# Stores of the normalised pairs issued from ScalarE's queue instead of SyncE's, in a fused graph-layer kernel

## What is computed

```python
msg  = x[src]
agg  = segment_sum(msg, dst)              # sum over the edges that end in a node
mean = agg / max(deg, 1)
h    = mean @ W_l + b + x @ W_r
y    = x + h * sigmoid(h)
out  = (y - mean(y)) / sqrt(var(y) + 1e-5)   # per node, over its 512 features
```

## Time and profile before

| what | value |
|---|---|
| median of 3 runs | 1533.49 us |
| the profiled execution's own time | 1532.49 us |
| its span, first to last instruction | 1530.7 us |
| PE, DVE, ACT, POOL busy, share of the span | 98, 86, 77, 67% |
| mean granted TensorE clock | 0.995 |
| device memory traffic over the span | 309 GB/s |

### The profile page before, as it was taken

The page is one execution under the profiler, slowest core; times in us unless marked ns, Lnnn a source line. Parts: engine busy times, 40 slices in busy tenths (PEclk is TensorE's granted clock), DMA queues, the critical chain, the costliest instruction groups (busy, mean ns, idle before and its releaser), DMA issues.

```text
span 1530.7 us, 23969 instructions
## 1 busy us (share of the span) xinstructions
PE 1498.7 (98%) x7198; PEld 1240.8 (81%) x7198; DVE 1320.3 (86%) x2090; ACT 1180.0 (77%) x1603; POOL 1025.4 (67%) x1089
## 2 busy tenths in 40 slices
PE   8999999999999999999999999999999999999996
PEld 6887778888888778888888888888888888888885
DVE  7988999999997878888888888888888888887886
ACT  5454333333334889999999999999999999999997
POOL 6446566666662766766767767667777777777774
PEclk9999999999999999999999999999999999999998
DMA  6476688989987789999989999999999999999996
GB/s 208 156 223 189 203 253 266 267 260 264 268 267 214 205 251 287 287 276 278 276 263 298 274 283 282 277 280 270 277 285 270 279 275 288 289 274 270 291 271 199
DMA packets 299349, 397.68 MB, mean 260 GB/s; under 512 B 43036, under 2 KB 145206, under 8 KB 299221
## 3 DMA queue, kind: packets, MB, share of 16 engines
q1 hardware_dynamic: 252277, 321.93, 70.5%
q0 software_dynamic: 46944, 74.22, 18.0%
HBM read 333.87 MB, written 139.67 MB: 309 GB/s over the span
## 4 chain that ended last, share of the span: by engine, by line
PE 68%; ACT 8%; issue 8%; DMA 5%; DVE 5%; POOL 5%; SPq 0%; POOLq 0%; ACTq 0%; DVEq 0%
PE pH L546 61%; DMA cor<-correction_rows,node_idx 4%; PE pT L651 3%; PE pT L620 3%; ACT cor L755 2%; ACT O L808 2%; POOL cor L452 2%; ACT pH L823 1%; ACT Z L835 1%; POOL rstd L516 1%; POOL var_eps L513 1%; PE pT L557 1%; POOL light_cor L452 1%; DVE Z L914 1%; DVE xs L1102 0%
## 5 line engine op out<-in xcount | busy, mean ns | idle before, releaser
L452 POOL DMA_INDIRECT cor<-correction_rows,node_idx x347 | 396.1, 1141 | 241.6 <-ACT cor L755 138.7
L546 PE MATMUL pH<-ws_hi,x_hi 128*128 128x512 f32 x876 | 347.3, 396 | 6.2 <-ACT pH L823 2.5
L546 PE MATMUL pH<-ws_hi,x_lo 128*128 128x512 f32 x876 | 343.3, 392 | 0.0
L546 PE MATMUL pH<-ws_lo,x_hi 128*128 128x512 f32 x876 | 342.3, 391 | 0.0
L546 PE MATMUL pH<-wb_hi,x_hi 128*128 128x512 f32 x688 | 275.5, 400 | 1.4 <-DVE x_lo L1090 1.3
L546 PE MATMUL pH<-wb_hi,x_lo 128*128 128x512 f32 x688 | 268.3, 390 | 0.0
L546 PE MATMUL pH<-wb_lo,x_hi 128*128 128x512 f32 x688 | 267.9, 389 | 0.0
L808 ACT ACTIVATE O<-Z,shift,rstd 128x512 f32<-128x512 f32 x347 | 262.7, 808 | 2.0 <-DVE shift L1137 1.9
L1127 DVE BATCH_NORM_STATS2 stats<-Z 128x6 f32<-128x512 f32 x347 | 219.4, 674 | 0.0
L729 ACT ACTIVATE s_hi<-sums 128x512 fp32r<-128x512 f32 x98 | 62.1, 634 | 196.8 <-issue 163.7
L1119 DVE TENSOR_TENSOR Z<-Z,X 128x1024 f32<-128x1024 f32 x174 | 211.3, 1214 | 1.1 <-ACT Z L835 1.1
(11 more groups left out here) (147 smaller groups left out, 2758.5 us busy)
## 6 DMA issues: line engine op xcount, KB each, us to landing
X<-in_x SPq DMA_DIRECT2D x173, 512.0 KB
out<-O SPq DMA_DIRECT2D x173, 512.0 KB
xs<-in_x SPq DMA_DIRECT2D x344, 128.0 KB
correction_rows<-c_out SPq DMA_DIRECT2D x98, 256.0 KB
light_x<-in_x SPq DMA_DIRECT2D x51, 256.0 KB, 2.9
light_h<-early_product SPq DMA_DIRECT2D x44, 256.0 KB
out<-light_o SPq DMA_DIRECT2D x44, 256.0 KB
join_row<-joined SPq DMA_DIRECT2D x98, 64.0 KB
```

What stands on the lines that cost most here:

```text
L452: g.indirect_dma_start(out=out_, out_offset=None, in_=table, in_offset=bass.IndirectOffsetOnAxis(ap=idx, axis=0), bounds_check=bound, oob_ ...
L546: last = mm(ps, a[:, k], w[:, k], start=(n == 0 and not onto), stop=(n == len(terms) - 1), skip_group_check=onto)
```

## The change

The function `store_out` moves, with its wait, from SyncE's block to ScalarE's. SyncE issued the store of pair t-3 in step t, after X's load. ScalarE issues the store of pair t-4 in step t, after the seed of pair t+1 and before `reset_cor` of pair t+3. At that place the normalisation of pair t-4 is the last instruction of ScalarE's step before. Behind the last step the stores stand between what is left of the normalisations.

```diff
 # SyncE
-            def store_out(t, q, u):
-                nt, rows = pair_shape(t)
-                b = u % 2
-                wait(sp, normed, t + 1)
-                if nt == 2:
-                    sp.dma_start(out[bass.ds(BASE + t * 2 * P, 2 * P), :].rearrange("(a p) n -> p a n", p=P), O[:, b]
-                                 ).then_inc(stored[b], 16)
...
                 shifted(t, q, u, 3, NP, load_x)
-                shifted(t, q, u, -3, NP, store_out)
                 lights(light, t)
             peeled(0, NP, move)
-            single(NP - 3, store_out)
-            single(NP - 2, store_out)
             last_lights(light)
-            single(NP - 1, store_out)
 # ScalarE
+            def store_out(t, q, u):
...
+                wait(act, normed, t + 1)
+                if nt == 2:
+                    act.dma_start(out[bass.ds(BASE + t * 2 * P, 2 * P), :].rearrange("(a p) n -> p a n", p=P), O[:, b]
+                                 ).then_inc(stored[b], 16)
...
                 if t + 1 >= ADDED:
                     shifted(t, q, u, 1, NP, seed)
+                shifted(t, q, u, -4, NP, store_out)
                 shifted(t, q, u, 3, NP, reset_cor)
                 lights(light, t)
                 shifted(t, q, u, -3, NP, normalise)
             peeled(0, NP, node_pair)
+            single(NP - 4, store_out)
             single(NP - 3, normalise)
             single(NP - 1, silu)
+            single(NP - 3, store_out)
             single(NP - 2, normalise)
             last_lights(light)
+            single(NP - 2, store_out)
             single(NP - 1, normalise)
+            single(NP - 1, store_out)
```

More of the change, by code:

```diff
@@ L353, in load_blocks @@
                                  ).then_inc(blocks_in, 16)
-            def store_out(t, q, u):
-                nt, rows = pair_shape(t)
-                b = u % 2
-                wait(sp, normed, t + 1)
-                if nt == 2:
-                    sp.dma_start(out[bass.ds(BASE + t * 2 * P, 2 * P), :].rearrange("(a p) n -> p a n", p=P), O[:, b]
-                                 ).then_inc(stored[b], 16)
-                else:
-                    sp.dma_start(out[BASE + t * 2 * P:N, :], O[0:rows, b, 0]).then_inc(stored[b], 16)
             def load_light(l):
@@ L835, in silu @@
                 a_(Z[0:rows, b, 0:nt], h, ACT.Silu).then_inc(silu_made, 1)
+            def store_out(t, q, u):
+                nt, rows = pair_shape(t)
+                b = u % 2
+                wait(act, normed, t + 1)
+                if nt == 2:
+                    act.dma_start(out[bass.ds(BASE + t * 2 * P, 2 * P), :].rearrange("(a p) n -> p a n", p=P), O[:, b]
+                                 ).then_inc(stored[b], 16)
+                else:
+                    act.dma_start(out[BASE + t * 2 * P:N, :], O[0:rows, b, 0]).then_inc(stored[b], 16)
             def light_make_silu(l):
```

## The result

The changed kernel takes 1528.32 us (median of 10 runs, 1527.06 to 1529.98) against 1532.14 us for the kernel before (10 runs, 1529.29 to 1535.54): ratio 0.9974, interval 0.9966 to 0.9982. Three more measurements on other occasions gave 0.9976, 0.9977 and 0.9979. So it is faster by 0.21 to 0.26%, some 3 to 4 us. In the last of these measurements 2 of 12 executions of the changed kernel took 1724 and 1879 us at a mean granted clock of 0.82 and 0.75 instead of 0.995, and are left out of its ratio. The forecast of 1533.7 us was wrong, in its sign as in its range.

A forecast was written before the change was run, and what follows sets the result against it. PE's pace through its instruction list was taken to bound the pair stage, with ScalarE second at 0.23 us slack a step. Terms 0 + 0 + 0 + 0.2 us on the 1533.5 us median gave 1533.7 us, range 1529 to 1548.

The forecast's parts named there:

- The issue on ScalarE: In each ScalarE step, issuing the store takes about 0.40 us beside the rounding and costs 0 compute.
- the wait on `normed`: On ScalarE's queue behind the seed, the store's wait for its normalisation is already met and costs nothing.
- The end: After the last pairs, a store breaks four normalisations by 0.5 to 0.9 us, partly hidden; cost 0 to 0.3, taken 0.2 us.
- the cover: At the last pair, VectorE's work before the last residual at 1521.84 us hides 0.7 us of silu's delay.
- the first rival: In the pair stage, issuing stores stops ScalarE's compute: +30 us, 1563 us, chance 0.09.
- Removed from SyncE: SyncE's queue loses 174 waits and issues, 70 us; earlier loads gain 0 to 0.2 us, taken as 0.
- The store leaves later: ScalarE issues each store 0.9 us later, leaving 8.3 us to land; cost 0 to a few tenths, inside the slack.
- One ring becomes two: With stores and loads in separate DMA rings, each gather lands 0.2 us later, taken up by slack; PE: 0.
- The rival by the ring's share: Later gathers stall PE one to four more times: +4 to +17 us, about 1542 us, chance 0.21.
- The faster rival: The early PE stall at 541 to 552 us vanishes, saving 4.3 us: 1529.4 us, chance 0.13.

The follow-up runs named there:

- mixed kernels: Changed kernel with stores issued early, behind silu, in one kind of step: only without block loads, ratio 0.9977; only with block loads, 1.0001.

## Why the prediction was wrong

**The issue on ScalarE** was right: free beside the rounding, 0.38 us where 0.40 was assumed. So was that the wait on `normed` costs nothing at this place. The end came out a little better than the 0.2 us that I took: the gap of 0.51 us is there, but from pair 173 to the end both kernels need 21.4 us (22.1 in one profile of the kernel before). I had misread the cover: silu of the last pair ends at 1520.30, 1.54 us before the residual at 1521.84, not 0.7 us. The price of the first rival, 30 us, was half of what an open issue costs, 60 us; in the changed kernel it did not arise.

**The step that failed is "Removed from SyncE ... the gain is 0 to 0.2 us. I take 0", together with "The store leaves later" and "One ring becomes two ... +0.2 us per gather".** Measured, the gain was 3 to 4 us, and the seeds waited less for gathers, 1.8 instead of 5.8 us. The step had two faults.

The first is a reading. I took PE's 0.2 us wait for X and its busy time of 919.78 us as proof that PE lost nothing in the long stage. The same list of waits had a row for PE's weight loads, which I left out:

```profile
PEld pT L651 <- DMA X<-in_x: 1.3, 3, 0.6
```

A modelled busy time does not show a late start that is under a few tenths. By the starts of the transposes the stage had lost 0.8 us in that profile, 2.5 in another. The first 16 pairs lost more, and I counted that as one event, not as part of the stage.

The second is the mechanism. I priced the store's move by what is taken away from SyncE, by packets in a ring, and its later departure only by the buffer that it frees. That it then no longer enters ahead of the block loads I put at nothing, without a word. Store and blocks are 512 KB each, by an estimate from 279 GB/s 1.9 us each. In the kernel before the store went ahead of the blocks in 77 of 78 steps; in the changed one ScalarE's queue comes to it only when silu has ended and the seed's gather has landed, and it goes behind the first of them in 75 of 78. The mixed kernels show that this place decides, for two rings: 0.9977 against 1.0001. That the gathers and X are late because they meet store and blocks together is argued from the waits (18.1 us for gathers against 1.3), and not shown by itself.

**The rival by the ring's share** (gathers a third instead of a half) did not come, and the effect had the other sign: in the changed kernel the seeds wait for gathers 1.0 to 2.6 us, before 5.8 to 11.6. One ring and two rings with the store behind the blocks take the same time (0.9978 and 0.9977), so the effect of one more ring is too small to see. The Trainium skill, "DMA: Bandwidth & Descriptors", section "Queues, rings and completion order", has the round-robin rule behind this rival; no run here shows whether it holds. The Trainium skill, "DMA: Bandwidth & Descriptors", section "Issuing engines are not separate DMA queues", says that issuing from several engines only saves issue time; that comparison agrees.

**The faster rival**, with a chance of 0.13 and 1529.4 us, came nearest in time. That the number came near is in part luck. Its mechanism was half right: the early stall is a late gather, and in the changed kernel it lands in 6.0 to 7.0 us instead of 7.2 to 8.8. But it is no fixed event of 4.3 us: that double step cost 1.2 to 4.4 us over PE's pace in three profiles of the same kernel, and small losses stand along the whole stage, beside seeds and X that are late.

**Open:** why in one ring both orders are needed, while in two rings the store's place beside the blocks is enough; and why in two rings it is enough to be 0.5 us behind the first block load, with the other three still to come. The waits show what is late in each case (gathers or X), not how the DMA engines divide themselves. Also open is how the rest of the difference between timed executions spreads over places that a profile of another execution shows; the account of parts rests on three and four profiles.

## What to carry to other kernels

When an engine looks busy all the time and its ends are modelled, measure the distance between equal instructions of successive steps, and compare it with the smallest that occurs: here a loss of 0.2% showed there, while PE's busy time was the same to 0.1 us. A store's ring and issuing engine mattered less here than what it goes ahead of: try a bulk store behind the loads and gathers that someone waits for, and measure it, since behind the block loads alone it gave nothing in one ring. An engine that computes all the time can issue a transfer for nothing, if the computing instructions that its queue has already handed over last longer than the issue. Directly behind the instruction whose result it stores the issue cost 60 us.

## What had not been expected of the hardware

- Four issues of 128 KB in a row on ScalarE's queue took 617 ns each by the median, 1648 at most; one issue of 512 KB took 378 ns. So fewer bytes did not make an issue shorter; what made these longer was not tested.
- A second ring for the stores (42514 packets, 23.6% of the DMA engines' time) moved neither the time nor the rate, against one ring with the stores behind the loads: 1529.81 against 1530.24 us, 280 against 279 GB/s. The busy share of the DMA engines was lower, 0.92 against 0.96, for the same transfers.
- The same kernel, from the same instruction on, needed 1036.0, 1039.0 and 1040.1 us in three executions. One profile is not enough to place a loss of 0.2%.
